# A gated graph network on one core: edge sums at the head of the step, r·hn ahead of the new state, the residual sum inside the state update

## The reference, cut to what matters

```
for l in range(4):                         # x: 50000 nodes x 128
    m   = x @ weight[l]
    agg = segment_sum(m[src], dst)         # 75000 edges, 50000 of them self loops, sorted by dst
    gi, gh = agg @ w_ih.T + b_ih, x @ w_hh.T + b_hh     # each split in r, z, n
    r = sigmoid(i_r + h_r); z = sigmoid(i_z + h_z)
    n = tanh(i_n + r * h_n)
    x = (1 - z) * n + z * x                # computed as z * (x - n) + n
out = layernorm(x_0 + (x + x_0))           # x_0: the input; over the 128 features, no affine part
```

## Time and profile before

| | |
|---|---|
| three runs | median 2386.39 us (2386.11 to 2389.70) |
| profiled execution, its own time | 2389.03 us |
| its span, first to last instruction | 2387.2 us |
| busy in the span | TensorE 94%, its weight loads 80%, VectorE 86%, ScalarE 77%, GpSimd 71% |
| mean granted TensorE clock | 0.988 of 2.4 GHz |
| chain that ended last | TensorE 55%, VectorE 21%, ScalarE 12%, issue 8% |

### The profile page before, as it was taken

One profiled execution on the slowest core, in us unless ns is written; L12 is line 12 of the kernel. 1 busy time (PEld: TensorE's weight loads), 2 busy tenths in 40 slices (PEclk: granted clock), 3 DMA queues, 4 the chain that ended last, 5 costly groups with the idle time before them and its releaser, 6 DMA issues.

```text
span 2387.2 us, 48608 instructions
## 1 busy us (share of the span) xinstructions
PE 2239.4 (94%) x11728; PEld 1906.8 (80%) x11728; DVE 2053.6 (86%) x3927; ACT 1833.7 (77%) x3483; POOL 1689.6 (71%) x1654
## 2 busy tenths in 40 slices
PE   3999999999899999999999999999988888988886
PEld 2888888888788888888788888888777777777774
DVE  7788888888688888888688888888779999998987
ACT  1688888888678888888678888888747777777776
POOL 3887777777487777777487777777477777777773
PEclk7999999999999999999999999999999999999998
DMA  2455555555456666666556666656534555554553
GB/s 56 123 160 160 161 160 159 162 157 161 121 162 171 171 171 168 172 172 167 146 146 172 171 167 172 172 167 169 168 100 135 145 142 144 141 145 141 147 142 109
DMA packets 277062, 362.43 MB, mean 152 GB/s; under 512 B 107754, under 2 KB 186586, under 8 KB 276980
## 3 DMA queue, kind: packets, MB, share of 16 engines
q1 hardware_dynamic: 238118, 309.12, 44.0%
q0 software_dynamic: 38784, 52.30, 9.7%
q10 hardware_dynamic: 78, 0.08, 0.0%
HBM read 208.71 MB, written 179.20 MB: 162 GB/s over the span
## 4 chain that ended last, share of the span: by engine, by line
PE 55%; DVE 21%; ACT 12%; issue 8%; DMA 1%; DVEq 1%; POOL 1%; ACTq 0%; POOLq 0%; SPq 0%
PE pZ L852 15%; PE pR L852 7%; PE pHN L852 7%; PE pA L840 7%; DVE diff L1457 4%; PE pO L939 4%; DVE diff L1451 4%; PE pA L852 4%; PE pIN L852 4%; DVE aggT L1414 3%; ACT o_rows L1132 3%; ACT a_hi L1083 3%; PE pR L893 2%; PE pR L896 2%; PE pR L894 2%
## 5 line engine op out<-in xcount | busy, mean ns | idle before, releaser
L688 POOL DMA_INDIRECT gath<-state,idx x900 | 932.7, 1036 | 267.0 <-issue 251.7
L665 POOL TENSOR_TENSOR h_lo<-hT,h_hi 128x250 fp32r<-128x250 f32 (+2 forms) x400 | 345.9, 865 | 286.2 <-DVE diff L1457 282.9
L1083 ACT CAST a_hi<-aggT 128x500 fp32r<-128x500 f32 x396 | 241.9, 611 | 330.8 <-DVE aggT L1414 330.8
L688 POOL DMA_INDIRECT gath<-in_x_dram,idx x300 | 320.4, 1068 | 101.8 <-issue 71.1
L1457 DVE TENSOR_TENSOR diff<-pZ,diff 128x500 f32<-128x500 f32 x400 | 271.4, 678 | 40.7 <-issue 0.5
L1096 ACT ACTIVATE rg<-pR,bsum 128x500 f32<-128x500 f32 x400 | 270.3, 676 | 44.2 <-PE pR L896 26.8
L1405 DVE TENSOR_TENSOR a_lo<-aggT,a_hi 128x500 fp32r<-128x500 f32 x396 | 269.1, 680 | 5.4 <-ACT a_hi L1083 4.7
L1078 ACT CAST sel<-sel 128x504 fp32r (+1 forms) x400 | 244.2, 611 | 31.7 <-DVE flag_i L1388 29.6
L1414 DVE TENSOR_TENSOR aggT<-pA,hT 128x500 f32<-128x500 f32 x396 | 264.9, 669 | 3.3 <-PE pA L840 3.3
L1108 ACT ACTIVATE pZ<-pZ,bsum 128x500 f32<-128x500 f32 x400 | 257.4, 643 | 9.4 <-PE pZ L852 9.4
L852 PE MATMUL pZ<-a_hi,wf_hi 128*128 128x500 f32 x400 | 190.7, 477 | 66.2 <-DVE diff L1457 66.0
(11 more groups left out here) (215 smaller groups left out, 6323.1 us busy)
## 6 DMA issues: line engine op xcount, KB each, us to landing
columns<-newT SPq DMA_DIRECT2D x300, 250.0 KB, 2.7
hT<-columns SPq DMA_DIRECT2D x300, 250.0 KB, 2.7
state<-o_rows SPq DMA_DIRECT2D x300, 224.0 KB
x_rows<-in_x_dram SPq DMA_DIRECT2D x200, 224.0 KB
out_dram<-o_rows SPq DMA_DIRECT2D x91, 224.0 KB
gath<-state,idx POOLq DMA_INDIRECT x900, 2.5
state<-o_rows SPq DMA_DIRECT2D x297, 26.0 KB
idx<-edge_src SPq DMA_DIRECT2D x395, 1.5 KB
```

The lines of the kernel that those rows point to most:

```text
L665: nc.gpsimd.tensor_tensor(part_of(h_lo, u)[:, cols], hT[:, u % RING, cols], part_of(h_hi, u)[:, cols].bitcast(F32), ALU.subtract).then_inc ...
L688: pool.indirect_dma_start(out=gath[:, u % RING, j, :], out_offset=None, in_=states[l], in_offset=bass.IndirectOffsetOnAxis(ap=idx[:, u % R ...
L1083: nc.scalar.copy(by_rows(a_hi[:, u % RING, :]), sums_of if summed else by_rows(aggT[:, :])).then_inc(s_ahi, 1)
```

## The change

On VectorE `aggregate` of block b+1 stands at the head of step b (before: of b+2 in the middle of step b), and its high and low parts follow as parts of b+1. r·hn of b stands ahead of the new state of b-1. In the last layer the residual sum stands between h minus n and the product with z; the row statistics stay behind. A wait is added to `difference`: `diff` may only be overwritten once the new state before has read it. On ScalarE the high part of the sums of b+1 follows the n gate; rows out (layers 1 and 2) or the high part of the state (layer 0) go behind the r gate; `normalise` is one piece of four, ahead of the z gate, and its rule for the step after `shift` goes. TensorE, GpSimd and SyncE are not touched.

```diff
 ScalarE
-            def normalise(u, stored, shifted, part):
+            def normalise(u, stored, shifted):
...
-                for k in range(part * RPP // 2, (part + 1) * RPP // 2):
+                for k in range(RPP):
...
                         if exists_before(i, u, ADDED_APART + 1):
                             n_gate_in_place(l, *after(i, u, -1)[:2])
                         if not ramp:
-                            rows(i, u)
-                            high()
-                        fresh = half_done(i, u, OUTLAG) if final else None
-                        if not fresh:
-                            normal(i, u, 0)
-                        r_gate(l, b, u, first and l == 0)
-                        if fresh:
-                            normal(i, u, 0)
-                        if ramp:
-                            if u == 3:
-                                high_part(l, 4, 4)
-                            rows(i, u)
+                            if exists(i, u, 1):
+                                high_part(l, *after(i, u, 1)[:2])
+                            if l:
+                                high()
+                            else:
+                                rows(i, u)
+                        r_gate(l, b, u, first and l == 0)
+                        if ramp and u == 3:
+                            high_part(l, 4, 4)
+                        if ramp or l:
+                            rows(i, u)
+                        if ramp or l == 0:
                             high()
...
+                        normal(i, u)
                         if not seeded(i, u):
                             n_gate(u, l * ADDED_APART + b + 1)
...
-                        if not ramp and exists(i, u, 2):
-                            high_part(l, *after(i, u, 2)[:2])
                         z_gate(l, b, u)
-                        normal(i, u, 1)
 VectorE
-            def difference(l, b, u):
+            def difference(l, b, u, overwritten=None):
                 dve.wait_ge(s_n, l * NB + b + 1)
+                if overwritten is not None:
+                    dve.wait_ge(s_new, overwritten)
...
+                        if not ramp and exists(i, u, 1):
+                            aggregate(l, *after(i, u, 1)[:2])
                         if exists_before(i, u, ADDED_APART + 1):
-                            difference(l, *after(i, u, -1)[:2])
+                            difference(l, *after(i, u, -1)[:2], l * NB + b - 1)
+                            if added and not ramp:
+                                remainder(*after(i, u, -ROWLAG))
                             product(l, *after(i, u, -1)[:2])
+                        elif added and not ramp:
+                            remainder(*after(i, u, -ROWLAG))
+                        if onto:
+                            r_times_hn_below_in(l, b, u)
                         if onto or u:
                             renew(*after(i, u, -1))
...
-                        if onto:
-                            r_times_hn_below_in(l, b, u)
-                        else:
+                        if not onto:
                             r_times_hn(l, b, u)
                             n_argument(l, b, u)
...
-                        summed = after(i, u, 1 if ramp else 2)[:2] if exists(i, u, 2) else None
-                        if summed and not (ramp and u == 3):
+                        summed = after(i, u, 1)[:2] if exists(i, u, 1) and not (ramp and u == 3) else None
+                        if ramp and summed:
                             aggregate(l, *summed)
                         if added and not ramp:
-                            remainder(*after(i, u, -ROWLAG))
                             row_stats(*after(i, u, -ROWLAG)[:2])
...
-                        if summed and not (ramp and u == 3):
+                        if summed:
                             low_part(l, *summed)
```

More of the change, by code:

```diff
@@ L1124, in last_rows_out @@
                               o_rows[PARTS[1], u, :]).then_inc(s_store[u], 16)
-            def normalise(u, stored, shifted, part):
-                if part == 0:
-                    act.wait_ge(s_store[u % RING], 32 * stored)
-                    act.wait_ge(s_nmr, shifted)
-                for k in range(part * RPP // 2, (part + 1) * RPP // 2):
+            def normalise(u, stored, shifted):
+                act.wait_ge(s_store[u % RING], 32 * stored)
+                act.wait_ge(s_nmr, shifted)
+                for k in range(RPP):
                     last = nc.scalar.activation(o_rows[:, u % RING, k * D:(k + 1) * D], y_rows[:, u, k * D:(k + 1) * D],
                                                 ACT.Identity, bias=nmr[:, u, k:k + 1], scale=rstd[:, u, k:k + 1])
-                if part:
-                    last.then_inc(s_o, 1)
+                last.then_inc(s_o, 1)
             def normalise_in_place(u, shifted, columns):
@@ L1156, in rows, with normal @@
                             rows_out(l, pb, pu, earlier(turn(pi, pu)))
-                    def normal(i, u, part):
+                    def normal(i, u):
                         if final and exists_before(i, u, lag):
                             pb, pu, pi = after(i, u, -lag)
-                            normalise(pu, earlier(turn(pi, pu)), turn(pi, pu) + 1, part)
+                            normalise(pu, earlier(turn(pi, pu)), turn(pi, pu) + 1)
                     def step(i, u, first, last):
@@ L1208, in step @@
                             high_part(l, *after(i, u, 1)[:2])
-                        if not ramp and exists(i, u, 2):
-                            high_part(l, *after(i, u, 2)[:2])
                         z_gate(l, b, u)
-                        normal(i, u, 1)
                         if ramp and u != 1:
                             widen(l, {0: 2, 2: 5, 3: 6}[u], {0: 2, 2: 5, 3: 6}[u])
-                        if ramp and u == 3:
-                            high_part(l, 5, 5)
                         if opening(i) and not unsplit(l, b + 3):
@@ L1242, in one @@
                         else:
-                            for part in range(2):
-                                normalise(0, l * NB + b, b + 1, part)
+                            normalise(0, l * NB + b, b + 1)
                     one_by_one(act, one)
@@ L1579, in step @@
                             low_h(*coming[:3])
-                        if summed and not (ramp and u == 3):
+                        if summed:
                             low_part(l, *summed)
-                        if ramp and u == 3:
-                            aggregate(l, 5, 5)
                         if not onto:
@@ L1589, in step @@
                             variance(*half)
-                        if ramp and u == 3:
-                            low_part(l, 5, 5)
                         if opening(i) and not unsplit(l, b + 3):
@@ L1599, in step @@
                         if last:
-                            difference(l, b, u)
+                            difference(l, b, u, l * NB + b)
                             product(l, b, u)
```

## The result

The changed kernel takes 2499.95 us (2499.14 to 2503.21, 4 runs) against 2387.89 before (2386.11 to 2389.70, 4 runs): 1.0471 times as long, interval 1.0455 to 1.0488. The forecast was 2460 with a range of 2430 to 2502. Direction and main cause came out; the loss was 112 us where 74 had been summed. The measured time lies outside the forecast's own range of 2430 to 2490. It is inside the full one only because that was widened for rivals A (2497) and B (2491), and neither of these happened, so the hit on the range is in part luck.

What follows compares the result with a forecast made beforehand. TensorE's own list was taken to bound layers 0 to 2, a loop through ScalarE and VectorE layer 3. +111 and -37 gave +74 on 2389.03, 2463, less 2.64 to the median: 2460 us; range 2430 to 2490, with A and B 2502.

Steps and rivals of the forecast that it cites:

- Rival A: Layer 3 gains nothing, its steps stay at 6.28 us: 2497 us in total, chance 0.13.
- Rival B: A held transposes' start on TensorE gives nothing back, 0.55 instead of 0.43: 2491 us in total, chance 0.10.
- The loop: Layers 0 to 2: last r matmul, r gate, held r·hn, new state, transposes' load at M + 2.65; +111 us.
- mark: Also M: the start of TensorE's last r matmul of a step, from which the forecast counts times in us.
- Rival C: Not slower: new state is in time, TensorE feels no wait, only layer 3's gain is left; 2349 us, chance 0.06.
- What a held start gives back: TensorE's held transposes: load to next load 0.43 instead of 0.55 us, so 0.12 us a step back.
- Moved with it, set at nothing: Other moved pieces (aggregate, low and high parts, rows out, GpSimd, added wait) cost nothing; r gate still at M + 0.49.
- Layer 3, the gain: Layer 3: the loop over high part and n gate is cut, 5.85 us a step, -0.43 for 87 steps, -37 us.
- the shift's step: Layer 3: four normalise pieces wait for the shift ahead of z gate and next n gate; some 0.4 us lost.
- The step with moments: Layer 3: VectorE has 0.70 us more work, 0.6 late after slack; 0.2 us lost on TensorE.
- The ordinary step: Layer 3: held by TensorE itself at 5.73 us, with VectorE's list at 5.63 just under it.
- the two limits level: Layer 3: held transposes at M + 2.65, with 0.12 back, come out level with TensorE's own order; no loss.

Runs made afterwards that it cites:

- The part alone: The kernel before with only r·hn put ahead of the new state on VectorE (with the added wait in difference): 2520.01 us, 1.0551 of before.
- 13 us by the experiment: The changed kernel with the high part of the state back ahead of the r gate in layer 0, rows out behind it: 2487.28 us, 1.0417 of before.
- the columns moved away: The changed kernel with layer 3's whole low part of the state on GpSimd (500 columns instead of 350, 150 on VectorE): 2489.86 us, 1.0431 of before.
- the state first: The changed kernel with r·hn back behind the new state in all layers, the rest of the change kept: 2392.63 us, 1.0025 of before.
- the kernel that is faster than both: The changed kernel with r·hn back behind the new state and layer 0's high part of the state ahead of the r gate: 2341.91 us, 0.9818 of before.

## Why the prediction was right or wrong

**The loop, right.** Each link came out as the row of before had it: 0.49, 0.78, 0.65, 0.72 for 0.73, the transposes at mark + 2.64 for 2.65. The part alone gave 6.11, 5.70 and 5.68 where 6.12, 5.67 and 5.67 had been worked out, and taking it back removed the loss in layers 1 and 2. Rival C (the state is in time) is out.

**What a held start gives back, right.** 0.43 to the next load, as at the single held place of the earlier trace rows, and the next mark 3.04 behind the transposes' load instead of 3.16, both in the mean over layer 1: 0.12. Rival B is out. What fails with it is how I had applied the rule of the Trainium skill (TensorE: Matmul & The Clock Gate, Architectural detail) that the queue can pull weight loads ahead of matmuls in flight. The exposed load is there, as the second transpose starts 0.21 behind the held first one against 0.11 where nothing is held. But a load taken early started 0.22 ahead of its own transpose, since the last z matmul stood between them, and that is gone at the held start: 0.22 - (0.21 - 0.11) = 0.12.

**"Moved with it, set at nothing", wrong in layer 0.** The step that failed is the one on the high part of the state, with the r gate that "still starts at M + 0.49" behind it: it was checked for whether the r gate and TensorE get it in time, and GpSimd was said to wait for the product alone. GpSimd's low part waits for the high part as well, and that was moved behind the r gate: 99.3 us of waiting, and its piece starts 1.45 us after the end of the product (397.10 to 398.55) instead of right behind it. It then lies beside `select`, which takes 1.55 us instead of 0.67, and through aggregate and high part of the sums this delays the r gate to M + 0.65 in the mean: 13 us by the experiment.

**Layer 3, the gain half as large.** -18.6 for -37. Behind the opening, five steps took 30.24 us where 29.25 had been summed. The term that was too small is the shift's step: +0.4 in the sum, +1.2 measured (6.9 to 7.0 against 5.73), and 0.8 in each of 16 such steps makes 13 of the 18 us. The step with moments took 6.07 for 5.93. In the shift's step VectorE's 150 columns take 1.59 us beside GpSimd's piece, and low part, aggregate and difference come 1.3 us later. The n gate, which I had taken for what is late next, was ready at 2211.67 while difference came at 2212.39. With the columns moved away this step took 6.1 to 6.2, as summed, but the step behind it grew, so the experiment does not give the price of the collision by itself.

The ordinary step has the right number by the wrong limit. It took 5.72 to 5.79 for the 5.73 that I had called TensorE's own. But with the state first many of these steps take 5.49 for the same products, so TensorE's own list is no longer than that, and the step of the earlier trace rows had some 0.24 of waiting in it. In the changed kernel the loop of layers 1 and 2 holds layer 3 as well, with 2.70 to the transposes' load and 3.04 from there to the next mark in the mean of two of the three ordinary steps:

```profile
2195.69 0.75 DVE L1433 SCALAR_TENSOR_TENSOR pIN<-pHN,bhh,rg 128x500 f32<-128x500 f32 x1 [0.32 <-ACT rg L1096]
...
2196.35 0.67 DVE L1461 TENSOR_TENSOR newT<-diff,pA 128x500 f32<-128x500 f32 x1
...
2197.07 0.51 PEld L939 LDWEIGHTS pH<-ident,newT 128*125 128x125 f32 x4 [0.44 <-DVE newT L1461]
```

The forecast had the two limits level, and so took r·hn ahead to be free in this layer; its experiment gives 7 us.

There is also a gap that I did not count. With aggregate at the head it stands right behind the low part that reads the same tile, and waits for it:

```profile
2186.41 0.67 DVE L1398 TENSOR_TENSOR a_lo<-aggT,a_hi 128x500 fp32r<-128x500 f32 x1
...
2187.27 0.68 DVE L1407 TENSOR_TENSOR aggT<-pA,hT 128x500 f32<-128x500 f32 x1 [0.19 <-DVE a_lo L1398]
```

0.86 from start to start (0.71 in the middle of 70 cases) instead of 0.59. What this gap costs was not tried. Rival A (layer 3 gains nothing) is out.

**Layers 1 and 2 before the change were not quite TensorE's list.** The windows view showed 448.00 busy of 448, and I took 5.28 for TensorE's own. With the state first and the rest of the change it is 5.19, so 0.09 a step had been waiting that does not show as idle. It lies at the z product, which waits for `product`: before, `product` ended at M + 0.83, the first z matmul started at M + 0.89 and the second 0.32 behind it. With the state first `product` ends at M + 0.55, and the two stand at M + 0.86 and 0.26 behind (means of layer 1). It did not touch the sum, as the new loop is longer than either, but it is why the kernel that is faster than both gains 18 us in those two layers.

**The parts of the change, then.** On the profiled executions, with the rest of the change in place, r·hn ahead of the new state costs layer 0 47 us (563.2 to 609.7), layers 1 and 2 46 and 45 us (518 to 564, 520 to 565) and layer 3 7 us. Alone on the kernel before it costs layers 1 and 2 only 37 and 35, as that kernel had not yet gained what the rest gives. The high part behind the r gate, with rows out ahead of it, costs 13 in layer 0, and 49 when the state is first. The residual sum in between gives 10 in layer 3. The rest was not taken apart: the head place of the aggregate, the high part of the sums behind the n gate, rows out behind the r gate and, in layer 3, `normalise` in one piece give some 18 together there (620.9 to 602.4) and 9 in each of layers 1 and 2.

## What to carry to other kernels

When one engine's piece is moved ahead of another, follow what the moved-back piece was feeding, up to the next event of the piece moved ahead: here state, transposes, next products, next gate, a loop whose length could be added up from single rows. A busy share of 100% does not say that a list has no slack; compare its step with the step of a kernel in which nothing is held. And check a list of pieces for what runs beside it on a neighbour engine as well as for what it waits for, as a piece that is in time may still land beside another and double it.

## What the runs showed of the hardware

A VectorE operation with both inputs in the on-chip memory (SBUF) took 0.9 to 1.3 us more in four places where it met GpSimd's subtraction on that memory: `select` 1.55 for 0.67, the low part of the gathered rows 1.62 for 0.55, 150 columns 1.59 for 0.30, and 125x20 elements 1507 ns for 189. The extra is set by when GpSimd's piece ends. The slow pieces end 0.54, 0.42, 0.18 and 0.06 us behind it (medians), in each case 0.12 or 0.13 less than their own undisturbed duration, as if they did their work only once GpSimd's piece was done. Pieces with one input in the matmul banks beside it (`product`, r·hn, new state) kept 0.67 to 0.75. It can also be GpSimd's piece that waits, as its 1.80 us beside an unchanged `select` show. The Trainium skill, SBUF — State Buffer, Who interferes with whom, states this as an exclusive lock on a port pair that VectorE and GpSimd share, held for a whole instruction, and gives as one of its cases a VectorE operation with two inputs there against a GpSimd operation that reads there. The runs agree with the rule on which pieces are slow: all four have two inputs in SBUF, so it could have named them in advance, and the prediction did not ask. No run isolates the lock itself. Which side waits can't be read from the starts in the profile, as the 150 columns start 0.45 us ahead of GpSimd's piece (2209.59 and 2210.04) and are the ones that grow.

A VectorE piece that waits for one of ScalarE started 0.10 after its end in r·hn's case (999.95 + 0.68 to 1000.73). A piece on VectorE behind one that it depends on started 0.1 to 0.3 later than one that does not (0.78 against 0.59 in the earlier trace rows, 0.71 to 0.86 against 0.59 for the aggregate).
